# Two pairs of each edge loop gather rows of x itself, ahead of the node tables

## What is computed

```python
h = jnp.maximum(_layernorm(x, axis=-1), 0.0)
# layer 0: attention over the edges of each destination
xl = h @ Wl + bl;  xr = h @ Wr + br;  e = edge_attr @ We
m = jax.nn.leaky_relu(xl[src] + xr[dst] + e, 0.2)
logits = m @ att                       # softmax over the edges of one dst
out = segment_sum(xl[src] * alpha[:, None], dst)
x = x + batch_norm(gelu(h + out + bias_out))
# layer 1
h = jnp.maximum(_layernorm(x, axis=-1), 0.0)
em = relu(layer_norm(concat([h[src], h[dst]]) @ msg_w + msg_b))
messages = segment_sum(em * edge_weights[:, None], dst) / counts
gate = sigmoid(h @ gate_w + gate_b)
h_new = relu(layer_norm(concat([h, messages]) @ upd_w + upd_b))
x = x + gate * h_new + (1 - gate) * h
```

## Time and profile before

| | us |
|---|---|
| median of 3 runs (lowest, highest) | 2365.58 (2364.89, 2366.14) |
| the profiled execution, its own time | 2365.31 |
| its span, first to last instruction | 2363.5 |

### The profile page before, as it was taken

How to read it: one execution, slowest core, us unless ns; L and a number is a source line. 1 busy time by engine, 2 the same in 40 slices (tenths; PEclk the granted TensorE clock), 3 DMA queues, 4 the chain that set the end, 5 groups by cost and what they waited for, 6 DMA issues and landing times.

```text
span 2363.5 us, 44525 instructions
## 1 busy us (share of the span) xinstructions
PE 1640.5 (69%) x9934; PEld 1199.2 (51%) x9934; DVE 1533.3 (65%) x4997; ACT 1022.4 (43%) x3829; POOL 1625.8 (69%) x1712
## 2 busy tenths in 40 slices
PE   6477778778787787878486666666666666656653
PEld 4255555555555565555365544454454454545542
DVE  6566565565655655655678776666766767666658
ACT  5244434344343443434444444444444434444437
POOL 4677777777777777776017777777777777777740
PEclk8699989898999988989578888887888879888786
DMA  8644443444444434443443443444434334343332
GB/s 207 177 95 90 93 93 87 94 94 89 93 89 93 93 88 94 90 91 75 130 122 81 96 93 86 94 88 93 93 87 93 90 89 91 88 93 88 93 94 64
DMA packets 206216, 228.63 MB, mean 97 GB/s; under 512 B 102602, under 2 KB 151775, under 8 KB 206093
## 3 DMA queue, kind: packets, MB, share of 16 engines
q0 software_dynamic: 55296, 115.25, 25.1%
q1 hardware_dynamic: 150190, 112.05, 17.0%
q10 hardware_dynamic: 672, 0.69, 0.1%
HBM read 194.60 MB, written 33.24 MB: 96 GB/s over the span
## 4 chain that ended last, share of the span: by engine, by line
POOL 57%; issue 20%; PE 8%; DVE 6%; DMA 6%; ACT 2%; POOLq 1%; SPq 1%; ACTq 0%; DVEq 0%
POOL room L693 57%; DMA room<-src_table,rec 4%; PE psum L726 1%; PE psum L862 1%; PE psum L801 1%; DVE stats L1222 1%; PE psum L867 1%; PE psum L773 1%; PE psum L783 1%; PE psum L768 0%; PE psum L880 0%; DMA b_lr<-in_L_gnn_br 0%; ACT room L1153 0%; DMA room<-state 0%; PE psum L896 0%
## 5 line engine op out<-in xcount | busy, mean ns | idle before, releaser
L693 POOL DMA_INDIRECT room<-src_table,rec x1664 | 1596.3, 959 | 604.2 <-issue 498.0
L862 PE MATMUL psum<-room,ident 128*128 128x384 f32 (+1 forms) x512 | 296.5, 667 | 355.5 <-DMA room<-src_table,rec 319.1
L1107 ACT ACTIVATE room<-psum 128x128 f32<-128x128 f32 x832 | 219.4, 275 | 558.3 <-DVE room L1607 549.0
L1424 DVE TENSOR_TENSOR room<-psum,room 128x384 f32<-128x384 f32 (+1 forms) x256 | 151.0, 590 | 395.1 <-ACT room L1039 263.4
L1039 ACT ACTIVATE room<-psum 128x384 f32<-128x384 f32 (+1 forms) x256 | 131.5, 514 | 541.3 <-PE psum L773 533.3
L1607 DVE TENSOR_TENSOR room<-psum,msg_g 128x384 f32<-128x384 f32 (+1 forms) x256 | 150.4, 588 | 300.5 <-PE psum L867 296.4
L862 PEld LDWEIGHTS psum<-room,ident 128*128 128x128 f32 x512 | 93.6, 228 | 378.8 <-issue 303.3
L867 PEld LDWEIGHTS psum<-room 125*128 125x128 bf16 x2496 | 201.2, 114 | 148.6 <-issue 127.5
L801 PE MATMUL psum<-room 128*125 128x128 f32 x1664 | 261.5, 299 | 16.9 <-ACT room L1057 11.4
L880 PE MATMUL psum<-room 128*125 128x128 f32 x1664 | 269.7, 306 | 1.9 <-ACT room L1119 1.9
L768 PE MATMUL psum<-room 128*128 128x384 bf16 (+1 forms) x768 | 188.4, 356 | 91.2 <-DVE room L1416 51.5
(11 more groups left out here) (203 smaller groups left out, 2156.7 us busy)
## 6 DMA issues: line engine op xcount, KB each, us to landing
room<-dst_perm SPq DMA_DIRECT2D x128, 406.2 KB
room<-src_table,rec POOLq DMA_INDIRECT x1664
room<-dst_table SPq DMA_DIRECT2D x128, 62.5 KB
src_table<-rows SPq DMA_DIRECT2D x24, 224.0 KB
dst_table<-rows SPq DMA_DIRECT2D x24, 224.0 KB
st_in<-state SPq DMA_DIRECT2D x64, 64.0 KB
state<-st_out SPq DMA_DIRECT2D x64, 64.0 KB
st_in<-state SPq DMA_DIRECT2D x64, 62.5 KB
```

The costliest lines, as they stand in the source:

```text
L693: pool.indirect_dma_start(out=xg[:, u, t * P:(t + 1) * P], out_offset=None, in_=src_table[n][:, :], in_offset=bass.IndirectOffsetOnAxis(ap ...
L862: nc.tensor.matmul(msg_bank[b][:, cols], ident[:, :], xg[:, u, t0 * P:t1 * P], start=True, stop=False, skip_group_check=True)
L1107: i = nc.scalar.activation(sq[:, j * P:(j + 1) * P], msg_bank[b][:, j * P:(j + 1) * P], ACT.Square, accum_out=var_e[:, c, j:j + 1])
```

## The change

`RAW` = 2 pairs of each loop (pairs 0 and 1) no longer gather rows of `src_table`. In loop 1 they gather rows of the input x, in loop 2 rows of a new DRAM copy of the layer's input, `x1_rows`, which SyncE stores group by group as it is made. Those rows are then normalised, turned, multiplied and given their bias on the chip, in place in `xg`: pair 0 ahead of the loop, pair 1 spread over the slots of pair 0 and the first slot of pair 1 (`raw_second`).

For that, source numbers of pairs 0 and 1 must be known before the list is: the list now begins with one item each for chunks 0 and 1, and has their remaining windows, if any, after them (`NI` = `NCH` + 2 items). The sum of pairs stays what it was.

The opening is dealt anew. Source numbers and weights go from DRAM to DRAM (SyncE) instead of by way of the chip; POOL loads the destinations with a conversion to float; POOL makes the permuted destinations and the three bf16 parts of the weights, after its 26 gathers; ScalarE loads the records of pairs 2 and 3; VectorE takes all statistics of x before the first bias; 14 of the 16 other weights are loaded after the gathers of loop 1.

The own part of layer 1 now computes all 50 gate columns by one-column products, does 4 groups before loop 2 and the other 9 in slots 1 to 3 of it, with one of VectorE's passes now on ScalarE (`own_rest`).

```diff
+RAW = 2
...
+            for k in range(RAW):
+                sp.dma_start(rec[:, k, 0:T].bitcast(I32), a["src"][k * CH:(k + 1) * CH].rearrange("(p t) -> p t", t=T)).then_inc(gat.rec[k], 16)
...
-            for f in (0, 2):
-                load_field(sp, f)
+            for c, e, v in chunk_rows(a["edge_weight1"].rearrange("e a -> (e a)")):
+                sp.dma_start(raw_w[c, e], v).then_inc(s_weights, 16)
+            for f, v in ((0, a["src"]), (2, a["edge_weight"])):
+                to = rec_rows.bitcast(I32) if f == 0 else rec_rows
+                zeros = zero_row.bitcast(I32) if f == 0 else zero_row
+                for c, e, rows_v in chunk_rows(v):
+                    sp.dma_start(to[c, f, e], rows_v).then_inc(s_rec, 16)
+                sp.dma_start(to[FULL_CH:NCH, f, REST_E:CH], zeros[:, :]).then_inc(s_rec, 16)
+            for to, v in other_weights:
+                sp.dma_start(to, v).then_inc(s_wb, 16)
+            sp.wait_ge(s_dst, 48)
+            sp.dma_start(rec_rows[:, 1, :], dst_f[0:NCH, :]).then_inc(s_rec, 16)
...
             for g in range(NG):
-                if g == 9:
-                    sp.wait_ge(s_counts, 1)
-                    blocks = block_count(sp)
-                    last = pair_count(sp)
-                    sp.wait_ge(s_rec, 6 * 16)
-                    sp.wait_ge(s_list, 16)
-                    first_records(0, gat)
                 store_rows(0, g)
                 if g == 6:
+                    sp.wait_ge(s_we, 1)
+                    for v in range(2):
+                        sp.dma_start(dws[W:P, v, :, :], we_part[0:P - W, :, :]).then_inc(s_weout, 16)
+                if g == 10:
                     sp.wait_ge(s_blk3, 1)
                     sp.dma_start(pair_list[0:P, :], lout).then_inc(s_list, 16)
-            sp.wait_ge(s_dpout, 32)
+                if g == 11:
+                    sp.wait_ge(s_dperm, 1)
+                    sp.dma_start(dst_perm[:, :], dperm[0:NCH, :]).then_inc(s_dpout, 16)
+            sp.wait_ge(s_counts, 1)
+            blocks = block_count(sp)
...
             sp.wait_ge(s_ewp, 4)
-            for c0, c1 in STORE_ROWS:
-                sp.dma_start(ew_perm[c0:c1, :, :], ewp[c0:c1, :, :]).then_inc(s_ews, 16)
-            sp.wait_ge(s_ews, 32)
+            sp.dma_start(ew_perm[:, :, :], ewp[0:NCH, :, :]).then_inc(s_ews, 16)
+            sp.wait_ge(s_ews, 16)
...
+            for g, (t0, t1) in enumerate(GROUPS):
+                sp.wait_ge(s_x1, g + 1)
+                for p0, p1 in NODE_ROWS:
+                    sp.dma_start(node_cols(x1_rows, p0, p1, t0, t1), node_x[p0:p1, t0:t1, :]).then_inc(s_x1_out, 16)
...
+            for c, e, v in chunk_rows(a["dst"]):
+                pool.dma_start(dst_f[c, e], v).then_inc(s_dst, 16)
...
+            def gather_pair(n, s, k, u):
+                pool.wait_ge(s.rec[u], turns(s, k, u, U, 16, last))
+                first_rows = type(k) is int and k < RAW
+                table = (a["x"], x1_rows)[n] if first_rows else src_table[n]
...
+                    for t in range(t0, t1):
+                        pool.indirect_dma_start(
+                            out=xg[:, u, t * P:(t + 1) * P], out_offset=None, in_=table[:, :],
+                            in_offset=bass.IndirectOffsetOnAxis(ap=rec[:, u, t:t + 1].bitcast(I32), axis=0),
+                        ).then_inc(s.xg[u][b], 16)
...
+            last = 0
+            for k in range(RAW):
+                gather_pair(0, gat, k, k)
...
+            pool.wait_ge(s_dst, 48)
+            pool.tensor_copy(dperm[0:NCH, :].rearrange("c (t p) -> c t p", t=T),
+                             dst_f[0:NCH, :].rearrange("c (p t) -> c t p", t=T)).then_inc(s_dperm, 1)
+            pool.wait_ge(s_weights, 48)
+            ew = raw_w[0:NCH, :].rearrange("c (p t) -> c t p", t=T)
+            left = ewl[0:NCH, :].rearrange("c (t p) -> c t p", t=T)
+            high = ewp[0:NCH, 0, :].rearrange("c (t p) -> c t p", t=T)
+            pool.tensor_copy(high, ew).then_inc(s_ewp, 1)
+            pool.wait_ge(s_ewp, 1)
+            pool.tensor_tensor(left, ew, high, ALU.subtract).then_inc(s_ewp, 1)
+            pool.wait_ge(s_ewp, 2)
+            pool.tensor_copy(ewp[0:NCH, 1, :], ewl[0:NCH, :]).then_inc(s_ewp, 1)
+            pool.wait_ge(s_ewp, 3)
+            pool.tensor_tensor(ewp[0:NCH, 2, :], ewl[0:NCH, :], ewp[0:NCH, 1, :], ALU.subtract).then_inc(s_ewp, 1)
...
+            tables_stored(0)
+            def first_slot(k, u, end):
+                if type(k) is not int or k >= RAW:
+                    gather_pair(0, gat, k, u)
+            all_pairs(pool, first_slot, last, 0)
+            for to, v in last_weights:
+                pool.dma_start(to, v).then_inc(s_wc, 16)
...
+            pool.wait_ge(s_x1_out, NG * 32)
+            def second_slot(k, u, end):
+                if type(k) is int and k == RAW:
+                    tables_stored(1)
+                gather_pair(1, msg, k, u)
+            all_pairs(pool, second_slot, last, 0)
...
+        def raw_first(pe, n, weights):
+            raw_turn(pe, n, 0, 0)
+            for b in range(NB):
+                if b + 1 < NB:
+                    raw_turn(pe, n, 0, b + 1)
+                raw_project(pe, n, 0, b, weights)
+        def raw_second(pe, n, k, b, weights):
+            if type(k) is int and k == 0:
+                raw_turn(pe, n, 1, b)
+                if b > 0:
+                    raw_project(pe, n, 1, b - 1, weights)
+            if type(k) is int and k == 1 and b == 0:
+                raw_project(pe, n, 1, NB - 1, weights)
...
+                    raw_second(pe, 1, k, b, msg_wc)
+                    if own_group(k, b) is not None:
+                        update_own(own_group(k, b))
                     lagged(msg_sums, k, u, b, 3, end)
...
+            pe.wait_ge(s_wc, NWC * 16)
+            for t in range(NT):
+                i = nc.tensor.matmul(own_gates[:, t:t + 1], feat_h[:, t, :], upd_w[:, D:D + 1], start=True, stop=True)
+            i.then_inc(s_u, 1)
+            pe.wait_ge(s_row, NGX + NG)
+            raw_first(pe, 1, msg_wc)
+            for g in range(OWN_FIRST):
                 update_own(g)
-            pe.wait_ge(s_zh, NG)
+            pe.wait_ge(s_zh, OWN_FIRST)
+            pe.wait_ge(s_gate, 1)
             all_pairs(pe, msg_slot, last, 1)
...
+            def raw_norm(n, r, b):
+                act.wait_ge(s_norm_scale, raw_part(n, r) + 1)
+                for t in range(*BLK[b]):
+                    rows_t = xg[:, r, t * P:(t + 1) * P]
+                    i = nc.scalar.activation(rows_t, rows_t, ACT.Identity, bias=raw_nmr[:, r, t:t + 1], scale=raw_rstd[:, r, t:t + 1])
+                i.then_inc(s_norm, 1)
...
+            def raw_second(n, k, b):
+                if type(k) is int and k == 0:
+                    raw_norm(n, 1, b)
+                    if b > 0:
+                        raw_features(n, 1, b - 1)
+                if type(k) is int and k == 1 and b == 0:
+                    raw_features(n, 1, NB - 1)
...
-            weights_part(0)
-            weights_part(1)
+            act.wait_ge(s_rec, 9 * 16)
+            act.wait_ge(s_list, 16)
+            load_rec(act, gat, 2, 2)
+            raw_deviations(0, 0)
+            for b in range(NB):
+                raw_features(0, 0, b)
+            load_rec(act, gat, 3, 3)
+            raw_deviations(0, 1)
...
+            def own_rest(g):
+                t0, t1 = GROUPS[g]
+                for t in range(t0, t1):
+                    i = nc.scalar.activation(node_h[:, t, :], node_h[:, t, :], ACT.Relu, scale=rest[:, t:t + 1])
+                i.then_inc(s_keep, 1)
...
+            def raw_scale(n, r, s):
+                for b, (t0, t1) in enumerate(BLK):
+                    dve.wait_ge(s.xg[r][b], turns(s, r, r, U, 16 * (t1 - t0), last))
+                    for t in range(t0, t1):
+                        dve.bn_stats(raw_stats[:, r, t, :], xg[:, r, t * P:(t + 1) * P]).then_inc(s_stats, 1)
...
+            def raw_rows(n, r, b, bias):
+                t0, t1 = BLK[b]
+                nt = t1 - t0
+                dve.wait_ge(s_proj, raw_group(n, r, b) + 1)
+                dve.tensor_tensor(xg[:, r, t0 * P:t1 * P].rearrange("p (j f) -> p j f", f=D),
+                                  raw_bank(r, b)[:, 0:nt * P].rearrange("p (j f) -> p j f", f=D),
+                                  bias[:, 0:D].unsqueeze(1).to_broadcast([P, nt, D]), ALU.add).then_inc(s_row, 1)
...
+            def raw_second(n, k, b, bias):
+                if type(k) is int and k == 0 and b > 1:
+                    raw_rows(n, 1, b - 2, bias)
+                if type(k) is int and k == 1 and b < 2:
+                    raw_rows(n, 1, b + 2, bias)
...
-            tables(0, b_lr, {0: opening, 1: lambda: x_stats(3), 2: later_columns, 3: chunk_spans, 6: count_pairs,
-                             7: lambda: list_block(0)})
-            edge_row_parts()
-            rest_of_weights(0)
-            rest_of_weights(1)
+            last = 0
```

(26 more changed lines are left out.)

405 lines of the change are left out of this document (224 added, 181 removed).

## The result

| | before | changed |
|---|---|---|
| median (lowest, highest), us | 2365.86 (2364.89, 2367.36), 4 runs | 2383.26 (2380.54, 2385.81), 4 runs |
| span of the profiled execution, us | 2363.5 | 2384.0 |

The changed kernel is slower: ratio 1.007, 95% interval 1.0058 to 1.0082, so 17.4 us more where 44 less were forecast. The forecast was wrong in sign, and 2383 lies outside its range.

What follows compares the result with a forecast made beforehand. GpSimd's gathers were taken as the bound, each loop's end set by when they begin and how many there are. From 2365.3, 22.9 us off loop 1 and 21.3 off loop 2 gave 2321 us, range of 8 in 10 2294 to 2346.

Steps and rivals of the forecast that it cites:

- 57 + 24 + 31 = 112: Loop 1: last table row at 57, first message 24 us later, pair 0's first sums 31 later; pair 4 gathered at 112.
- Ceiling and place of the limit: Both loops: 26 fewer gathers each save at most 33.6 and 34.5 us; pair 4 first needs a slot that consumers free.
- The last table row: Opening: last row of the table at 57 us, before 63.0, with fewer transfers and VectorE and ScalarE losing passes.
- From the last table row to the first message: Opening: VectorE's remaining work sums to 23, taken as 24 us, four bias passes with their chain 3.6; first message at 81.
- Slot 0 of loop 1: Raw turns of pair 1 wait for ScalarE's normalisation, 2.2 us a block; slot lengthens from 12.1 to 21 us.
- Between the loops: Before loop 2: pair 2 gathered at 1229 old time, 3 late; first message kept at 1255, bounds −5 and +8.
- Slot 0 of loop 2: Raw turns of pair 1 between pair 0's blocks add some 3.2 us a block; slot goes from 14.3 to 27.
- slots 1 to 3: Loop 2: three groups of the own part in each make them 18, 19.5 and 18 us, above GpSimd's 16.4.
- Pair 8 behind pair 4's first message: Loop 2: pair 8 waits only for pair 4's first block, 2 us after slots 0 to 3; 1340 old time, before 1361.30.
- My rival on the slower side: GpSimd's queue makes the edge weights late, delaying pair 4 to 161 in the worst case: 2370 us; chance 0.05.
- My lower bound for loop 1: Loop 1 gains only 6 us if gathers take 2.41 and passes 30 us, first message at about 98.
- The opening is no shorter: Rival: DMA bounds the first 45 us, first message at 89, loops gain 15 and 11 us: 2339 us; chance 0.21.

Runs made afterwards that it cites:

- f1: Changed kernel with asserted bounds, VectorE's passes over the destinations moved early into the opening's statistics: 2373.86 us, ratio 1.0029 to before.
- f6: Changed kernel with early destination passes, pair 1's normalisations ahead of loops, early loop 2 records, 34 gate products in slot 0, later attention columns: 2337.51 us, ratio 0.9861 to before.
- f2: Changed kernel with asserted bounds, pair 1's 13 normalisations on ScalarE moved ahead of each loop: 2372.92 us, ratio 1.0026 to before.
- f3: Changed kernel with asserted bounds, SyncE loading the record of pair k+4 in slot k of loop 2: 2370.16 us, ratio 1.0011 to before.
- h4_gates: Changed kernel with asserted bounds, 34 of 50 one-column gate products moved into slot 0 of loop 2: ratio 1.0136 to before, on a slow chip.

## Why the prediction was wrong

Pair 4 of loop 1 was to be at 57 + 24 + 31 = 112 and is at 71.3 + 31.8 + 35.0 = 138.1. Pair 8 of loop 2 was to be at 1317 and is at 1379.8. By its steps:

- **Ceiling and place of the limit: right.** Gathers leave at 1.26 us each, and pair 4 is the first to wait, for the sums. GpSimd's opening was right to 3 us.
- **The last table row, 14.3 us off.** I took 6 us less than before, and it is 8.3 more. GpSimd's passes were costed by their own length and as hidden; what they do to VectorE beside them was not asked. The `chunk_spans` passes stood still for 8.4 us; f1, which also moves 3.9 us of reductions, gives 9.4 back. "SBUF — State Buffer" of the Trainium skill (section "Who interferes with whom") says that a VectorE instruction with two SBUF inputs and a GpSimd instruction that reads SBUF exclude each other, whichever is second waiting until the first ends. The trace agrees, with ends within 0.03 us; one-input passes (0.15) and bias passes with one input from PSUM (1.29 for two) ran through. I weighed the page on the length of the passes and not the one on this lock. The 6 us of relief hoped for from fewer transfers showed only in f1, as 1 us (61.9 against 63.0).
- **From the last table row to the first message, 7.8 off.** The four bias passes with their chain took 9.2 us where I had 3.6: TensorE began behind the attention columns, and VectorE waited 4.58 us for the first product. With the columns moved, in f6, that wait is 1.29 us and the stretch 5.7 shorter than in f1. Registers and the list block took 1.3 more than put down, the rest is small.
- **Slot 0 of loop 1, 4.0 off.** The mechanism was right (the turn waits for ScalarE, 2.22 us at the first block), the size too small; f2 takes it to 19.4 us. What the sum lacked is the 3.60 us that the turn of the third block waits for VectorE's bias pass, and any term for TensorE's clock.
- **Between the loops, right to 0.5, then 8.7 off.** Against the last gather of loop 1, pair 2 came 3.5 later, where 3 was put down. But the products for the gate took 19.4 us, 0.39 each, on TensorE, ahead of the raw turns, and I had kept the first message in place; with 34 of them gone, in f6, that stretch is 8.8 us shorter.
- **Slot 0 of loop 2, 4.7 off; slots 1 to 3 right,** 54.0 us where I had 55.5.
- **Pair 8 behind pair 4's first message, 24.6 off.** This is the largest. I let a gather wait only for its slot of rows. It also waits for its record, and SyncE loads that in the slot after, behind the last message of the pair four before, and behind a store of sums that VectorE makes late in the slot. Before, the issues stood 22 us or more ahead of the gathers and the rule was hidden; with consumers late and gathers early it became the wait. The code of SyncE's slot says it; I had not followed that queue. f3 shows it.

The steps add up: 14.3 + 7.8 + 4.0 = 26.1 for loop 1, which come out as 26.7 at its last gather; 8.7 + 4.7 − 1.5 + 24.6 = 36.5 for loop 2. Pair 8 itself is 62.7 off, 0.5 under the sum of both because the forecast rounds its 1339.5 up to 1340. With 2 us that the rest of the loop drifted, that is the 2384.0 − 2363.5 + 44.2 = 64.7 by which the span misses the forecast.

My rival on the slower side had another mechanism (late edge weights); VectorE waited for none of them. My lower bound for loop 1 did not even keep that rival's rule: with gathers to 67 and passes of 30 us, 97 + 12.9 + 31 puts pair 4 at 141, which loses 6 us, and I wrote −6. "The opening is no shorter" was half right, but its 2339 had neither lock nor records in it. Nor did the range.

## What to carry to other kernels

When work is taken from a saturated engine, the next thing that it waits for is found by listing every semaphore ahead of its instruction and following each to the queue that raises it, the small loads (records, indices) included; a wait that has never shown in a trace may lie 20 us behind. An idle engine is not free for elementwise work: look which two-input passes of VectorE run beside it. Here five edits, most of them moves of a few lines, together turned 0.7% slower into 1.4% faster.

## What the runs showed of the hardware

- A GpSimd pass that reads and writes SBUF holds VectorE's passes with two SBUF inputs until it ends: 0.15 us became up to 4.03. Passes with one SBUF input beside it were not held.
- GpSimd's passes over 64x1664: with one input 1.56 us contiguous and 3.1 strided; with two inputs 3.32 us contiguous and 4.16 with one of them strided.
- A float32 product of a 128x125 weight with one column costs TensorE 0.43 us at a granted clock of 0.50 (1.2 GHz) and 0.23 at 1.00 (2.4 GHz): nine of them took 3.88 and 2.08 us in `h4_gates`. In the changed kernel 50 took 19.4, at 0.50 to 0.57.
- Chips differ: the same kernel took 3,089 us on one and 2,366 on another. Gathers and VectorE's passes lasted equally long, TensorE's granted clock was lower (0.83 for 0.90 from 600 to 800 us), and idle times between instructions were longer. The cause was not found.
